# Steps of 256 positions, a second root bank and gate products placed anew in a two-layer ternary and recurrent kernel on one core

## The reference, cut to what matters

```python
x = x + s1(layernorm(x)) * silu(layernorm(x) @ ternary(weight).T + bias)
#   s1: s = silu(xn @ w_gate.T); the k smallest |s| of each row := 0; (s * (xn @ w_up.T)) @ w_down.T
...
h = xn @ Win.T + bin                               # 512 -> 64 channels
for l in range(4):
    y = silu(layernorm(h, l1w, l1b))
    h = h + sconv(y, p[l]) * scl                   # a complex decaying recurrence over the sequence
    y = layernorm(h, l2w, l2b)
    h = h + silu(y @ W1.T + b1) @ W2.T + b2        # 64 -> 256 -> 64
s = layernorm(h) @ Wout.T + bout
g = silu(xn @ (W + sum_e coeffs_e * scales_e * Bf_e A_e).T + bias)
x = x + s * g
```

## Time and profile before

| | us |
|---|---|
| median of three runs | 615.48 (615.32 to 616.04) |
| the profiled execution | 616.52 |
| its span, first to last instruction | 614.7 |
| PE busy | 589.6 (96%) |
| DVE busy | 480.9 (78%) |
| ACT busy | 339.5 (55%) |
| POOL busy | 181.6 (30%) |
| mean granted TensorE clock, share of full | 0.987 |

### The profile page before, as it was taken

How to read it: one execution, slowest core, us unless ns; L and a number is a source line. 1 busy time by engine, 2 the same in 40 slices (tenths; PEclk the granted TensorE clock), 3 DMA queues, 4 the chain that set the end, 5 groups by cost and what they waited for, 6 DMA issues and landing times.

```text
span 614.7 us, 8872 instructions
## 1 busy us (share of the span) xinstructions
PE 589.6 (96%) x2852; PEld 458.4 (75%) x2852; DVE 480.9 (78%) x949; ACT 339.5 (55%) x573; POOL 181.6 (30%) x305
## 2 busy tenths in 40 slices
PE   7998999999999999999999999999998989989995
PEld 6887887888888888888888888886765556555542
DVE  6999799898788788688878868777887666666655
ACT  5878387266528617743841873484853545445531
POOL 2333002001000100100100020279945666663345
PEclk9998999999999999999999999999999898999999
DMA  8821000210030030002003000281110000000025
GB/s 343 325 72 36 2 0 2 69 36 2 1 102 0 0 102 0 0 24 78 0 0 102 0 0 34 81 308 35 41 32 1 0 1 1 1 0 2 1 84 189
DMA packets 18011, 32.37 MB, mean 53 GB/s; under 512 B 4054, under 2 KB 4566, under 8 KB 17980
## 3 DMA queue, kind: packets, MB, share of 16 engines
q1 hardware_dynamic: 17980, 32.00, 15.2%
HBM read 24.63 MB, written 7.36 MB: 52 GB/s over the span
## 4 chain that ended last, share of the span: by engine, by line
PE 76%; DVE 10%; POOL 6%; DMA 2%; ACT 2%; issue 1%; SPq 1%; DVEq 0%; POOLq 0%; ACTq 0%
PE ps_b L1836 18%; PE ps_a L1836 18%; PE ps_a L1869 15%; PE ps_b L2104 4%; PE ps_b L1876 3%; POOL lnr L852 3%; PE ps_a L2118 3%; PE ps_t L1855 2%; POOL arena L273 2%; ACT y L1089 1%; PE ps_t L2112 1%; DVE xc L1607 1%; DVE junk_d L1302 1%; DMA arena<-in_f_w_t 1%; PE ps_a L2061 1%
## 5 line engine op out<-in xcount | busy, mean ns | idle before, releaser
L1302 DVE TENSOR_SCALAR_CACHE_REDUCE junk_d<-k_buf,cand 128x1376 int8<-128x1376 f32 x56 | 91.8, 1640 | 0.3
L970 ACT ACTIVATE junk_a<-k_buf,cand 128x1376 int8<-128x1376 f32 x56 | 80.5, 1437 | 0.6
L949 ACT ACTIVATE s_buf<-ps_a 128x1376 f32<-128x1376 f32 x16 | 21.1, 1319 | 95.9 <-PE ps_a L1836 91.4
L1869 PE MATMUL ps_a<-wd_hi,zt_hi 128*128 128x512 f32 (+1 forms) x176 | 71.9, 409 | 0.0
L1869 PE MATMUL ps_a<-wd_hi,zt_lo 128*128 128x512 f32 (+1 forms) x176 | 69.2, 393 | 0.0
L1869 PE MATMUL ps_a<-wd_lo,zt_hi 128*128 128x512 f32 (+1 forms) x176 | 68.9, 391 | 0.0
L776 POOL TENSOR_TENSOR xres<-xres,gate 128x512 f32<-128x512 f32 x12 | 22.3, 1861 | 130.6 <-DVE gate L1428 130.6
L1836 PE MATMUL ps_a<-wg_hi,xt_hi 128*128 128x512 f32 (+1 forms) x192 | 52.7, 383 | 1.9 <-DVE xt_lo L1203 1.8
L768 POOL TENSOR_TENSOR rstd<-var_eps,expo 128x2 f32<-128x2 f32 x7 | 4.9, 703 | 162.6 <-DVE var_eps L1215 162.6
L1836 PE MATMUL ps_a<-wg_lo,xt_hi 128*128 128x512 f32 (+1 forms) x192 | 51.3, 376 | 1.1 <-DVE wg_lo L1198 1.1
L1836 PE MATMUL ps_b<-wu_hi,xt_hi 128*128 128x512 f32 (+1 forms) x192 | 51.8, 378 | 0.0
(11 more groups left out here) (262 smaller groups left out, 1343.2 us busy)
## 6 DMA issues: line engine op xcount, KB each, us to landing
xres<-in_x SPq DMA_DIRECT2D x8, 512.0 KB, 3.4
out<-arena SPq DMA_DIRECT2D x16, 256.0 KB, 2.0
xin<-in_x SPq DMA_DIRECT2D x7, 512.0 KB, 3.9
x_scratch<-xres SPq DMA_DIRECT2D x6, 514.0 KB, 3.9
arena<-x_scratch SPq DMA_DIRECT2D x3, 1028.0 KB, 9.8
m_buf<-in_wg_t SPq DMA_DIRECT2D x2, 688.0 KB, 5.2
k_buf<-in_wg_t SPq DMA_DIRECT2D x2, 688.0 KB, 8.4
m_buf<-in_wu_t SPq DMA_DIRECT2D x2, 688.0 KB, 7.7
```

The lines of the kernel that those rows point to most:

```text
L949: act.activation(s_buf[:, t, :], ps_a[:].rearrange("p a n -> p (a n)")[:, 0:INNER], ACT.Silu).then_inc(s_ready, 1)
L970: act.activation(junk_a[:], k_buf[:, 1, :], ACT.Sign, bias=c, scale=-1.0, accum_out=below[:, 1:2]).then_inc(act_step, 1)
L1302: dve.tensor_scalar(junk_d[:], k_buf[:, 0, :], c, -float(DROP), ALU.is_lt, ALU.add, accum_out=e).then_inc(cnt_dve, 1)
L1869: last = pe.matmul(ps_a[:, t, :], zs, ws[0:rows, c, :], start=(c == 0 and n == 0), stop=(c == CHUNKS - 1 and n == 2))
```

## The change

The change has these parts.

- **Gate products.** `FILLS` has seven numbers a phase: the second one is a new place between the two `variances`. Phase 0 takes 21 (26 before), step 1 takes 17 (21 before), each of steps 2 to 7 takes 24 (20 or 21 before), step 8 takes 19 (as before), and the tail 7 (20 before).
- **Two sides.** `widen`, `normed`, `turn_imaginary`, `norm_out` for silu and `spread` work in two sides of 256 positions. The roots of the first side go to `bank2[c]`, those of the second to `bank1[c]`.
- **The norm of the feeding half.** `norm_out(n, d)` on ACT is gone. DVE's `normed_scaled` multiplies by the root and by the norm's weight in one instruction, and writes y itself. The norm's bias is put through W1 once, in step 1 (`norm_biases`: eight PE matmuls with one column out, and one DVE addition to `b1_c`), and `hidden` adds the sum.
- **Up products** are eight of 256 columns instead of four of 512.
- **Tables.** In each step POOL makes one of the three and DVE the other two, behind `fed`; in step 1 DVE makes two more in front of `widen(q)`.
- **Phase 0.** The means of w2 (`weight_means`, L1688 and L1695) stand behind phase 0 as a whole, `h_in(1)` in front of `hand_over`, tokens 12 to 15 together, and `project_in(1)` in front of the last 5 gate products of the phase instead of its last 9; the first two gate tiles take their high parts first.
- **First pair.** DVE's two `q_bias` go: ACT copies the ternary product out of PSUM (`q_out`) and POOL adds the bias; `up_project(1, 0)` waits for the copy. `xt_low(1, 0)` stands one `halve` earlier and `xt_low(1, 1)` behind `choose`, in front of `mask(0, 0)`. POOL's waits for counts are placed anew.
- **Tail.** Its gate products stand as 4, 3, 0 instead of 7, 4, 9; the gates of ACT and DVE move up by one tile.

```diff
-FILLS = ((0, 0, 0, 0, 0, 26),) + ((2, 5, 4, 6, 2, 2),) * 3 + ((2, 5, 4, 6, 2, 1),) * 4 + ((2, 6, 5, 0, 6, 0),)
+FILLS = ((0, 0, 0, 0, 0, 0, 21), (2, 3, 1, 5, 4, 2, 0)) + ((2, 3, 7, 5, 5, 2, 0),) * 6 + ((1, 3, 6, 3, 0, 6, 0),)
...
+            pool.wait_ge(bias_in, 16)
+            for t in range(2):
+                pool.wait_ge(q_out, t + 1)
+                pool.tensor_tensor(gate2[:, t, :], gate2[:, t, :], bias_b[:], ALU.add).then_inc(q_biased, 1)
...
                         if n == 4:
+                            for t in range(2):
+                                act.wait_ge(q_done, t + 1)
+                                act.activation(gate2[:, t, :], ps_b[:, t, :], ACT.Copy).then_inc(q_out, 1)
                             at_most_first(p)
...
                 halve(0, 3)
+                xt_low(1, 0)
                 halve(0, 4)
-                xt_low(1, 0)
                 halve(0, 5)
-                xt_low(1, 1)
                 halve(0, 6)
-                dve.wait_ge(bias_in, 16)
-                for t in range(2):
-                    q_bias(0, t, False)
                 dve.wait_ge(wd_l, N_LOW)
                 largest_under(0, 0, False)
                 choose(0, 0)
+                xt_low(1, 1)
                 mask(0, 0)
...
+            def normed_scaled(l, c, side):
+                dve.wait_ge(ln_bc[c], 4 * l + side + 3)
+                dve.wait_ge(ln_xc[c], l + 1)
+                dve.scalar_tensor_tensor(out=y[:, half_of(c, side)], in0=h[:, half_of(c, side)],
+                                         scalar=pcol(l, C_L2W), in1=root_bank(c, side),
+                                         op0=ALU.mult, op1=ALU.mult).then_inc(ln_y[c], 1)
...
+                    if phase == 1:
+                        norm_biases()
+                        tables_some(7, 9)
+                    for side in range(2):
+                        widen(q, c, side)
+                    for side in range(2):
+                        normed(q, c, side)
                     decay(l, c)
-                    widen(n, d)
-                turn_imaginary(l, c)
+                for side in range(2):
+                    turn_imaginary(l, c, side)
+                    if feeds:
+                        widen(n, d, side)
...
             def spread(q, c):
-                pe.wait_ge(ln_w[c], q + 1)
+                for side in range(2):
+                    pe.wait_ge(ln_w[c], 2 * q + side + 1)
+                    if q % 2 and side:
+                        pe.wait_ge(ln_xc[c], q // 2 + 1)
+                    for j in range(2):
+                        last = pe.transpose(root_bank(c, side)[:, j * P:(j + 1) * P],
+                                            sq[:, sc(c, 2 * side + j)], ident[:])
+                    last.then_inc(ln_bc[c], 1)
...
+            def up_units(l, c):
+                for m in range(2):
+                    for side in range(2):
+                        pe.wait_ge(ln_y[c], 4 * l + side + 3)
+                        for b in range(BATCH):
...
+                            made = pe.matmul(up_bank(c, u)[:, half_of(0, side)], w1[rows, l, m * P:(m + 1) * P],
+                                             y[rows, half_of(c, side)], start=True, stop=True)
```

More of the change, by code:

```diff
@@ L1664, in fed, with tables_some @@
                                          in1=h[:, cs(c)], op0=ALU.add, op1=ALU.add).then_inc(h_ready[c], 1)
+            def tables_some(first, last):
+                for n in range(first, last):
+                    if n < 6 * DEPTH:
+                        tables(dve, dve_passed, n // 6, n % 6, n % 6 + 1)
             def residual(m):
@@ L1760, in _ @@
                 if feeds:
-                    normed(n, d)
+                    for side in range(2):
+                        normed_scaled(k, d, side)
                 scan(l, c, True)
@@ L1780, in _ @@
             variance(2 * DEPTH, 0)
-            gate_lo(TILES - 3)
+            gate_lo(TILES - 2)
             variance(2 * DEPTH - 1, 1)
-            gate_lo(TILES - 2)
-            widen(2 * DEPTH, 0)
-            normed(2 * DEPTH, 0)
-            widen(2 * DEPTH - 1, 1)
             gate_lo(TILES - 1)
-            normed(2 * DEPTH - 1, 1)
+            for side in range(2):
+                widen(2 * DEPTH, 0, side)
+            for side in range(2):
+                normed(2 * DEPTH, 0, side)
+            for side in range(2):
+                widen(2 * DEPTH - 1, 1, side)
+            for side in range(2):
+                normed_scaled(DEPTH - 1, 1, side)
             output(0)
@@ L1797, in _ @@
             output(4)
-            widen(2 * DEPTH, 1)
+            for side in range(2):
+                widen(2 * DEPTH, 1, side)
             output(5)
-            dve.wait_ge(ln_bc[1], 2 * DEPTH + 1)
+            dve.wait_ge(ln_bc[1], 4 * DEPTH + 1)
             for j in range(4):
@@ L2174, in _ @@
             spread(0, 0)
-            for i in range(LOADED, LOADED + 2):
+            for i in range(LOADED, TILES):
                 tokens(i)
+            gates(2 * KH)
+            project_in(1)
             gates(KH + 1)
-            for i in range(LOADED + 2, TILES):
-                tokens(i)
-            gates(4)
-            project_in(1)
-            gates(9)
             for phase in range(1, PHASES - 1):
@@ L2218, in _ @@
             output(4)
[L2219 removed]
+            gates(4)
             output_bias(5)
             output(5)
[L2222 to L2223 removed]
+            gates(3)
+            last_spread()
             for m in range(6, 8):
```

186 lines of the change are left out of this document (105 added, 81 removed).

## The result

The changed kernel takes 611.13 us (median of nine runs, 610.24 to 613.78) where the one before takes 615.48 (nine runs, 614.83 to 616.59): a ratio of 0.9931, 95% interval 0.9917 to 0.9946. It is faster by 4.35 us; 9.0 were forecast, and 611.13 lies 0.3 above the range. The profiled execution took 611.92 with a span of 610.1, 4.6 less than before on both counts.

What follows compares the result with a forecast made beforehand. PE, busy 96% of the span, was taken as the bound, so only PE work removed or idle filled helps. 2.3 + 2.5 - 1.5 + 2.4 + 3.3 = 9.0 off 615.48 gave 606.5 us, range 602.5 to 610.8.

Steps and rivals of the forecast that it cites:

- four signs of being wrong: Centre to centre above 14.9; DVE small operations 1 us beside POOL; clock under 0.9 in three+ steps; up products over 2.5.
- First pair: DVE's path to the flag: bias additions 1.2, `xt_low(1, 1)` 0.6, held one-column operation 0.9, less 0.4: +2.3 us (1.2 to 3.3).
- rival 3: The first pair gains nothing, since POOL's two additions hold DVE's small operations: 608.8 us; chance 0.12.
- Between phase 0 and step 1: Five gate products fewer (1.15) and no 1.31 wait for `xs_lo`: +2.5 us (1.2 to 3.2).
- Step 1: Eight narrow matmuls 1.6, four gates fewer 0.9 back, DVE tables before widening idling PE: -1.5 us (0 to -3).
- Steps 2 to 7: PE work 13.9 plus 0.6 idle makes 14.5 us a step, none at half clock: +2.4 us (-3 to 5).
- The 0.50 in front of the up products: PE's 0.50 us idle in each step goes because ACT's `norm_out(n, d)` is off the chain.
- Tail: 13 gate products fewer (3.0) and gates one tile earlier on DVE and ACT (0.3): +3.3 us (2 to 4).
- Rival 1: Half clock in three of steps 2 to 7, 1.3 us each (0.8 to 1.57): 610.4 us; chance 0.17.
- rival 2: No idle time is left in steps 2 to 7, 13.9 us each: 602.9 us; chance 0.14.
- rival 5: Up products of 256 columns do not run side by side, some 1.5 us more a step: 618.5 us; chance 0.04.
- Rival 4: Idle time in steps 2 to 7 stays, 13.9 plus 1.54, 15.4 us a step: 611.9 us; chance 0.05.

Runs made afterwards that it cites:

- experiment on DVE's order: Changed kernel, but in step 1 DVE widens q's roots first, then makes its two extra tables, and adds norm biases behind q's products; 608.95 us, ratio 0.9871.
- tables in phase 0: The kernel with all four edits, but POOL makes step 1's two extra tables in phase 0 instead of DVE in step 1; 604.29 us, ratio 0.9764.
- all four edits: Changed kernel with step 1 widening before extra tables, norm biases behind `project_in(1)`, both n widenings before turns, one gate moved before steps 2-7's first variances; 601.79 us.

## Why the prediction was wrong

Two things make nearly all of the shortfall. In steps 2 to 7 a wait that the sum had at 0.3 was 0.97, which the experiments show; less an error the other way this makes 1.6 in six steps. And the sum put half clock in step 1 and step 8 at nothing beyond what the kernel before had, where the profiled execution had 0.9 and 1.5 us of it. Together with 0.35 in the last sums this is the 4.4. None of the four signs of being wrong came: centre to centre was 14.8, the small operations beside POOL's additions took 0.41 at most, the clock was under 0.9 in two steps, and the up products took 1.9. Only the tail's term left its own bounds (2 to 4).

**First pair, 2.3 forecast, 2.8 measured.** The sum over DVE's path, 1.2, 0.6 and 0.9 less 0.4, came out: DVE sends its flag at 58.87 instead of 61.18, 2.3 earlier. What the sum left out is that PE was the later of the two before. It came to the flag at 61.81, 0.6 behind DVE, and the experiment with `xt_low` as before shows PE as the path too. In the changed kernel DVE is the later one (PE waits 0.45 for the flag at 58.93). So the size is nearly right and the path was PE's at first, not DVE's. The 0.9 of the held operation did come back:

```profile
52.47 0.17 DVE L1330 SCALAR_TENSOR_TENSOR rise<-below,width_d 128x1 f32<-128x1 f32 x1
...
56.63 0.41 DVE L1371 TENSOR_SCALAR pick<-iota,rank 128x8 f32<-128x8 f32 x1
```

Beside POOL's two additions (54.04 to 57.00) one small operation took 0.41 instead of 0.23, so rival 3 did not happen.

**Between phase 0 and step 1, 2.5 forecast, 2.0 measured.** No wait for `xs_lo` is left, as foreseen; the term was 0.5 too large.

**Step 1, -1.5 forecast, -2.4 measured.** At the clock of before (0.89) the forecast holds: the same step 1, in the experiment with a gate product behind the spread, took 17.04 at 0.90, 1.5 more than 15.53. There the sixteen narrow records took 1.9 instead of 1.6, four gates fewer gave 0.9, and PE idled 1.5 where it had idled 0.9 before, 0.6 more, where I had 0.8. The 0.9 that is missing is the longer half clock, which I had only in the far end of the range; under it the narrow records take 2.9, since they start at 0.11 each and go on at 0.21. Whether the change makes it longer stays open: three traces of this step 1 have 0.81, 0.81 and 0.90. What I overlooked is that the idle time could be had back. The addition waits for the narrow records and pushes the tables and the widening behind them, in the order `norm_biases()`, `tables_some(7, 9)`, `widen`; with the widening first, or with the tables on POOL, PE does not wait there.

**Steps 2 to 7, +2.4 forecast, +0.8 measured.** This is the term whose working failed. "0.3 remains in front of the second spread" was 0.97, and the 0.25 in front of the variances was 0.24. With both gone a step of 24 gate products takes 13.55, so PE's own work is at most 13.55 and not the 13.9 that I worked out. 13.55, 0.97 and 0.24 make 14.76 where I had 13.9 and 0.6, so an error of 0.35 in the work hid part of the 0.6 in the waits. I had taken PE's busy time before, 13.06, for its work. A last gate product in front of an idle stretch shows what else is in it:

```profile
521.07 0.40 PE L2104 MATMUL ps_b<-weff_lo,xs_hi 128*128 128x512 f32 x1
```

Its row is 0.40 long, but gate products in a row start 0.23 apart, so 0.17 of the row is no work in PE's way. With three idle stretches in the step that is 0.5: 13.06 less 0.5, and 0.9 for four gate products more, is 13.5 (an estimate from these rows).

The mechanism is the one that the prediction named in half a sentence, "the second side of `normed_scaled` behind the turn": it is the widening in front of it that stood behind the turn, twice, with two waits for silu's sides and two transposition pairs apart. I priced the split as a gain of overlap, and read the new DVE order in the sections above without adding up its chain: product 0.43, silu 0.61, turn 0.43, widening 0.3, from the first spread on, and the second side 0.5 behind.

**The 0.50 in front of the up products** goes, but not because ACT is off the chain: the run with ACT's copy back has the same steps. Nor did the up products in halves or the tables on DVE move a step.

**Tail, +3.3 forecast, +1.4 measured.** Step 8 has a clock of 0.89 in the changed kernel's profiled execution, where it had 1.00 before. Where it ran at full clock, in the experiment on DVE's order and in five others, the stretch takes 35.6, 1.55 less and 2.9 less than before. So the sum's 3.3 was 0.35 too large, and the rest is clock. The 2.9 is not the gate products alone. Behind step 8's centring PE's last output products start 3.9 sooner in that experiment (26.3 instead of 30.2), 3.0 for the 13 gate products and 0.9 more, but 1.0 of it is lost behind PE. DVE's last sums run beside POOL's, as they did before; there the longest took 1.21, and now one that elsewhere takes 0.68 took 1.60. The rows of DVE and of POOL:

```profile
602.49 1.60 DVE L1704 TENSOR_TENSOR arena<-xt,arena 128x512 f32<-128x512 f32 x1
```

```profile
598.30 6.73 POOL L886 TENSOR_TENSOR arena<-xt,arena 128x512 f32<-128x512 f32 x5 [1.01 <-DVE xt L1709]
```

The section "SBUF: two separate sides" of the page "SBUF — State Buffer" in the Trainium skill has this case, two operands in SBUF on VectorE beside a GpSimd operation; the row agrees, 0.92 lost.

**The rivals.** Rival 1 (half clock in three more steps) had the price right: a step with it took 0.83 more where PE still had slack (the run with the gate behind the spread) and 1.55 more in step 8 where it had little, between the bounds of 0.8 and 1.57. But it named steps 2 to 7, where none fell in the profiled execution; what it should have named is step 1 and step 8. Rivals 2, 3 and 5 did not happen. Rival 4, the idle time staying, is nearest to what did in the steps: 0.97 and 0.24 of waiting stand where 1.54 of idle stood, most of it in another place. That its 611.9 lies beside 611.13 is luck, since it had 15.4 for a step, which took 14.76, and no half clock.

## What to carry to other kernels

When a chain is cut in two sides, write down the new order of the engine that serves both chains and add up the way to the last consumer: an operation of the second chain put between the sides of the first inherits each wait of the first. Here that cost 0.97 us in each of six steps, 5.8 in all, where those steps had gained 0.78, and one move of three lines gave it back. The busy time of the matrix engine is not its work: here it held 0.24 of a wait after the change, and 0.5 of row ends before. What the work is at most shows in a version of the kernel in which nothing is waited for. And a small addition that waits for another engine belongs behind, not in front of, what others wait for.

## What was not expected of the hardware

- The clock's half speed does not belong to a place of the program. One kernel (tables in phase 0) ran with spans of 598.5 us at a mean granted clock of 0.997 and of 605.0 at 0.986 on the same chip, and the changed kernel with 608.5 at 0.989 and 612.0 at 0.986. Three kernels that are the same up to the end of step 1 ran it at 0.81, 0.81 and 0.90, in 17.90, 18.29 and 17.04 us. With the norm biases early it was at full clock twice and at 0.80 once.
- A matmul record of one column and one of two cost the same 0.11 us at 2.4 GHz (eight of 128x2 start over 0.88 to 0.91), and one of one column starts 0.21 after the other at 1.2 GHz: sixteen took 1.94 at full clock and 2.90 where the clock fell under way.

```profile
466.65 1.94 PE L2157 MATMUL ps_t<-arena,w 64*128 64x1 f32 x16
```

(This row is from the kernel with all four edits.)
